# The shift's transfers issued from ScalarE's queue instead of SyncE's

## The reference

```python
xn = layernorm(x);  s = attn0(xn);  g = silu(ffn0(xn));  x = x + s * g    # ffn0: soft mixture, 8 experts, 64 slots each
xn = layernorm(x);  s = attn1(xn);  g = silu(ffn1(xn));  x = x + s * g    # ffn1: routed, 16 experts
# attention: 16 heads of 8, rotary q and k, causal
scores = einsum('bhqd,bhkd->bhqk', q, k) * 8 ** -0.5                      # masked above the diagonal
out = einsum('bhqk,bhkd->bhqd', softmax(scores), v)
```

## Time and profile before

| | us |
|---|---|
| median of 3 runs (lowest to highest) | 719.22 (716.24 to 719.84) |
| the profiled execution | 713.31 |
| its span, first to last instruction | 711.5 |
| busy: TensorE, VectorE, ScalarE, GpSimd | 616.2, 504.4, 455.0, 259.0 |

### The profile page before, as it was taken

The page is one execution under the profiler, slowest core; times in us unless marked ns, Lnnn a source line. Parts: engine busy times, 40 slices in busy tenths (PEclk is TensorE's granted clock), DMA queues, the critical chain, the costliest instruction groups (busy, mean ns, idle before and its releaser), DMA issues.

```text
span 711.5 us, 14086 instructions
## 1 busy us (share of the span) xinstructions
PE 616.2 (87%) x4988; PEld 293.0 (41%) x5052; DVE 504.4 (71%) x825; ACT 455.0 (64%) x908; POOL 259.0 (36%) x459
## 2 busy tenths in 40 slices
PE   0687399499988999999999999899999999999983
PEld 0455033245453555444352354432333333346632
DVE  7967588375775546888978978599988898843222
ACT  0463156266646688778766676687777777766781
POOL 5665021314300211687111106791132221116883
PEclk9788579799998999999999999999999999999997
DMA  5057431300551300306230444063331330200002
GB/s 175 0 180 156 125 121 40 68 1 31 139 156 41 71 28 4 95 23 189 75 91 18 81 116 126 2 180 125 71 85 33 80 67 18 53 2 1 1 0 60
DMA packets 33323, 52.09 MB, mean 73 GB/s; under 512 B 5832, under 2 KB 23912, under 8 KB 30696
## 3 DMA queue, kind: packets, MB, share of 16 engines
q1 hardware_dynamic: 31960, 50.74, 26.8%
q10 hardware_dynamic: 1296, 0.46, 0.2%
HBM read 37.29 MB, written 13.63 MB: 72 GB/s over the span
## 4 chain that ended last, share of the span: by engine, by line
PE 56%; DVE 13%; POOL 12%; ACT 6%; issue 6%; DMA 4%; SPq 2%; another core or an unknown queue 0%; POOLq 0%; ACTq 0%; DVEq 0%
PE ps L1319 52%; DVE maxes L1302 5%; ACT probs L1034 3%; DVE sine L1156 2%; POOL gate L550 2%; DMA qop<-shiftT 2%; SPq L736 2%; POOL probs L862 2%; PE ps L1534 1%; DMA F<-in_w 1%; POOL xn L550 1%; PE ps L1373 1%; POOL gate L907 1%; POOL gate L908 1%; POOL x L897 1%
## 5 line engine op out<-in xcount | busy, mean ns | idle before, releaser
L1302 DVE TENSOR_REDUCE maxes<-ps 128x2 f32<-128x1024 f32 (+2 forms) x288 | 338.6, 1220 | 91.1 <-PE ps L1319 89.5
L1034 ACT ACTIVATE probs<-ps 128x512 f32<-128x512 f32 x576 | 305.3, 605 | 110.0 <-PE ps L1319 68.5
L1319 PE MATMUL ps<-qop,kop 128*128 128x512 bf16 (+3 forms) x704 | 163.8, 327 | 22.4 <-DMA qop<-shiftT 9.3
L862 POOL TENSOR_SCALAR_AFFINE_SELECT probs<-probs 128x512 f32<-128x512 f32 (+1 forms) x160 | 83.8, 546 | 249.1 <-ACT probs L1034 249.1
L1319 PE MATMUL ps<-probs,vals 128*9 128x512 f32 (+3 forms) x1536 | 150.1, 493 | 4.9 <-POOL probs L862 3.1
L1319 PE MATMUL ps<-kmx,qmx 32*128 32x128 bf16 (+2 forms) x1280 | 101.9, 269 | 20.6 <-DMA qop<-shiftH 8.9
L1319 PEld LDWEIGHTS ps<-qop,kop 128*128 128x128 bf16 x768 | 60.2, 99 | 110.7 <-ACT probs L1034 50.0
L1319 PEld LDWEIGHTS ps<-kmx,qmx 32*128 32x128 bf16 x1280 | 38.1, 93 | 118.4 <-issue 66.4
L1319 PE MATMUL ps<-F 128*128 128x128 f32 (+2 forms) x640 | 76.9, 283 | 5.4 <-DMA F<-in_w 3.9
L1319 PEld LDWEIGHTS ps<-F 128*128 128x128 f32 (+2 forms) x640 | 69.2, 181 | 20.2 <-issue 16.3
L1319 PEld LDWEIGHTS ps<-probs,vals 128*9 128x9 f32 x1536 | 29.7, 90 | 60.5 <-issue 43.8
(11 more groups left out here) (158 smaller groups left out, 643.4 us busy)
## 6 DMA issues: line engine op xcount, KB each, us to landing
qop<-q_thirds SPq DMA_DIRECT2D x48, 192.0 KB
kop<-k_thirds SPq DMA_DIRECT2D x48, 192.0 KB
qmx<-q_thirds SPq DMA_DIRECT2D x16, 256.0 KB
kmx<-k_thirds SPq DMA_DIRECT2D x16, 256.0 KB
F<-in_w SPq DMA_DIRECT2D x16, 256.0 KB, 5.1
q_thirds<-third SPq DMA_DIRECT2D x8, 384.0 KB, 4.4
k_thirds<-third SPq DMA_DIRECT2D x8, 384.0 KB, 3.8
q_thirds<-third SPq DMA_DIRECT2D x8, 256.0 KB, 3.3
```

Source lines behind the costliest of these rows:

```text
L862: last = pool.affine_select(where, where, [[0, number], [1, P]], ALU.is_ge, 0.0, base=0, channel_multiplier=-1)
L1034: act.activation(probs[:, u % RING, :], bank(at), ACT.Exp, scale=SCALE).then_inc(s_cells_read, 1)
L1302: dve.tensor_reduce(dst, src, AX.X, ALU.max).then_inc(s_units_read[pair // 2], 1)
L1319: return pe.matmul(out_, lhsT, rhs, start=first, stop=last)
```

## The change

The branch for `shift` leaves SyncE's program. In ScalarE's it issues the same transfers, with the same source, destination and semaphore, after the copy; ahead of them ScalarE waits until its own copy is done (`s_cells_read`). The waits ahead of the copy are as before.

```diff
--- before.py
+++ after.py
@@ -759,16 +759,6 @@
                         sp.dma_start(qop[rows_i, r, :, :].rearrange("p h t -> p (h t)"), q_rows).then_inc(s_xload[r], 16)
                         sp.dma_start(kop[rows_i, r, :, :].rearrange("p h t -> p (h t)"),
                                      k_rows[D * i:D * i + 3 * D, :]).then_inc(s_xload[r], 16)
-                elif kind == "shift":
-                    n, part = arg
-                    sp.wait_ge(s_cells_read, CELL[what] + 1)
-                    if part == 2:
-                        for k in range(2):
-                            sp.dma_start(qop[KR + k:KR + k + 1, n % 2, :, :], shiftT[HG * TB * k:HG * TB * k + HG * TB, :]
-                                         ).then_inc(s_shift_in[k][n % 2], 16)
-                    else:
-                        sp.dma_start(qop[KR:KR + 2, n % 2, :, BANK * part:BANK * part + BANK], shiftH[:, part, :]
-                                     ).then_inc(s_shift_in[part][n % 2], 16)
                 elif kind == "ldw":
                     e, = arg
                     if e < 4:
@@ -1035,15 +1025,23 @@
                 elif kind == "shift":
                     n, part = arg
                     act.wait_ge(s_cells_full, CELL[what] + 1)
+                    r, last = n % 2, (n - 1) % 2
                     if n:
                         for half in range(2):
-                            act.wait_ge(s_shift_in[half][(n - 1) % 2], 16 * ((n - 1) // 2 + 1))
+                            act.wait_ge(s_shift_in[half][last], 16 * ((n - 1) // 2 + 1))
                     if part == 2:
                         act.activation(shiftT[:, :], bank(at)[0:2 * HG * TB, 0:P // 2].bitcast(BF16), ACT.Copy
                                        ).then_inc(s_cells_read, 1)
+                        act.wait_ge(s_cells_read, CELL[what] + 1)
+                        for k in range(2):
+                            act.dma_start(qop[KR + k:KR + k + 1, r, :, :], shiftT[HG * TB * k:HG * TB * k + HG * TB, :]
+                                          ).then_inc(s_shift_in[k][r], 16)
                     else:
                         act.activation(shiftH[:, part, :], bank(at)[0:2 * HG, 0:BANK // 2].bitcast(BF16), ACT.Copy
                                        ).then_inc(s_cells_read, 1)
+                        act.wait_ge(s_cells_read, CELL[what] + 1)
+                        act.dma_start(qop[KR:KR + 2, r, :, BANK * part:BANK * part + BANK], shiftH[:, part, :]
+                                      ).then_inc(s_shift_in[part][r], 16)
                 elif kind == "pvout":
                     n, half = arg
                     act.wait_ge(s_pv, summed(n, HALF_END[half]))
```

## The result

The changed kernel takes 721.2 us (median of 20 runs, 716.1 to 724.3), the kernel before beside it 716.7 us (20 runs, 713.6 to 720.0). The ratio is 1.007, 95% interval 1.0051 to 1.0089, so about 5.0 us slower. Forecast were 711.5 us and faster. The time lies inside the range (703 to 722), the direction is wrong.

A forecast was written before the change was run, and what follows sets the result against it. TensorE was taken to bound the kernel, with two shift-transfer stalls reachable. Gains of 7.0 + 7.4 + 0.8 = 15.2 us less 7.5 us on ScalarE gave -7.7 us: 719.2 to 711.5 us, range 703 to 722.

The forecast's parts named there:

- What bounds the kernel: TensorE sets the end; of its waits the change can reach only two, on the shift's transfers, 8.9 and 9.3 us.
- The two stalls: TensorE's waits for group 0's shiftH (8.9 us) and group 1's shiftT (9.3 us); with clock, 15.2 us to be gained.
- The landing beside a full queue: Shift transfers in ScalarE's queue take turns with SyncE's packets, adding 2.2 and 2.6 us to an undisturbed 1.9.
- First stall: Group 0, near 78 us: transfer issued at 74.8 instead of 80.17, landing at 79.2 instead of 86.23; 7.0 us gained.
- Second stall: Group 1, near 130 us: the pair lands at 129.6 instead of 137.02; 7.4 us gained, about 1.8 us waiting left.
- SyncE's queue: SyncE no longer stands at the shifts, so ready stores and loads can go earlier; effect on TensorE taken as zero.
- What it costs on ScalarE: Issues delay ScalarE's activations: six places at 0.95 us, six at 0.3, others nothing; 7.5 us lost.
- The clock: After the second stall TensorE's low clock costs 1.5 us; half recovered, 0.8 us, bounds -1.7 to +1.7.
- A: Stalls mostly stay: queues not served by turns, or ScalarE's issue held until SyncE's ends; +4.5 us, 715.5 to 723.7; chance 0.20.
- B: ScalarE comes to pace TensorE, its issue delays passing whole: 29 us against 15.2, +14 us, 733 us; chance 0.08.
- C: ScalarE's delay costs nothing and the stalls go whole: -16 to -19 us, 700 to 703 us; chance 0.14.
- D: The change does nothing because other work sets the pace behind the stalls; chance 0.06.

The follow-up runs named there:

- e8: Kernel before, SyncE issuing everything, with group 1's loads moved behind group 0's first shift and group 2's behind group 1's; ratio 0.9720, -20.1 us.
- e13: Kernel before with all shift transfers on ScalarE, SyncE held at each shift, and groups 1 and 2's loads waiting until the preceding shift's transfer landed; 0.9788, -15.2 us.
- e14: As e13, but only groups 0 and 1's shift transfers issued by ScalarE, the others by SyncE; ratio 0.9704 to the kernel before, -21.2 us.
- e1: Kernel before with only groups 0 and 1's shift transfers issued by ScalarE; ratio 0.9886, -8.2 us.
- e9: e1 with group 2's six loads cut into twelve, pieces of 1 KB instead of 8 KB; ratio 0.9896 to the kernel before, -7.5 us.
- e2: Kernel before with only group 8's shift transfers issued by ScalarE, SyncE not held; ratio 1.0091, +6.5 us.
- e6: Kernel before with only group 8's shift transfers issued by ScalarE, SyncE still waiting there for the copy; ratio 1.0024, +1.7 us.
- e4: The change with all transfers on ScalarE, but SyncE still waiting at each shift for the copy; ratio 0.9955 to the kernel before, -3.2 us.
- e3: Kernel before with only group 4's shift transfers issued by ScalarE, SyncE not held; ratio 1.0047, +3.4 us.
- e5: Kernel before with groups 9 to 15's shift transfers issued by ScalarE, SyncE held at those shifts; ratio 1.0061, +4.4 us.
- e12: Kernel before with groups 2, 3, 5, 6 and 7's shift transfers issued by ScalarE, SyncE held there; ratio 0.9982, -1.3 us.
- e11: e4 plus e8's order of loads, groups 1 and 2's behind the shifts; ratio 0.9955 to the kernel before, -3.2 us.

## Why the prediction was wrong

**What bounds the kernel: right.** The two stalls were the only waits that the change could take away, and they were worth more than I gave them: e8, which takes them both, gains 20 us.

**The landing beside a full queue: mis-sized, and the mechanism was wrong.** I priced it by turns of packets read at the start of the trace, 2.2 and 2.6 us on top of 1.9. First stall: 4.4 us expected from the end of the copy, 6.6 measured (75.77 to 82.33), near the far end of my bounds (6.1 to 7.0 us); TensorE's wait is 4.0 us where my sum left 1.3. Second stall: 4.5 us after the second issue expected, 8.8 measured; the wait shrank by 3.2 us, where my bounds began at 5. (The landing at 129.54 meets my 129.6 only because all of it stands 4.3 us earlier by then; TensorE's wait was to be about 1.8 us and is 6.1.) The issue while SyncE is stuck took 1.27 us, inside my bounds, but not because SyncE was stuck: the same issue takes 1.27 us in e13 and e14 too, where SyncE's issues ended over 1 us earlier. In all the term was to be 15.2 us and is 8.2 (e1), at the low end of my 8 to 19. The packets show the queues not taking turns (none of ScalarE's for 4.5 and 6.1 us), and in e9 a smaller piece didn't bring the landing forward; e13 and e14 show that 2.4 to 4.2 us is what such a transfer needs when the loads are held back (e13: 73.17 to 77.36 for group 0, 2.6 to 3.0 for group 1). The earlier trace rows had the queues side by side, but not the time of a small transfer under a full load; no row of before had it for a second queue, and I should have kept the 6 and 12 us that the rows do show as the likely value and not as the far end.

The Trainium skill, "DMA: Bandwidth & Descriptors", section "Issuing engines are not separate DMA queues", has the two engines' transfers interleave on the same 16 DMA engines, so that a second issuer saves only the issue. The runs agree in the main: 8.8 us against 12.4 us, where 2.8 was to be had. Its section "Queues, rings and completion order" also states that the count that reports a transfer lands only after every earlier write of that DMA engine, across its queues. I did not weigh this rule, and it spoke against the change. By the packets it is not what makes the transfers late here: at group 8 the ten packets themselves did not run for 6.1 of the 7.3 us, so a late count is at most the small rest. Why a queue has to wait so long for its turn no run here tells; that stays open.

**SyncE's queue, "I take zero": the step that turned the sign.** The prediction said that what is ready behind the shifts "can now go earlier" and stopped there. It asked whether TensorE waits for a group's load, and not what the earlier loads do to the transfer that they overtake. The wait at the shift was also what kept loads behind the shift. It costs 4.8 us at group 8 (e2 less e6, 1.9 to 7.7), 8.2 us between the change and e4 (6.3 to 10.2; 5.8 in their two traces). The row that would have warned was in hand: the earlier trace rows showed what six loads ahead of a shift do.

**What it costs on ScalarE: right in sum, not in place.** 7.5 us expected; 3.4 + 4.4 - 1.3 = 6.5 us from e3, e5 and e12, 8.2 with group 8's 1.7 (e6), which I had at nothing, and 6.0 (3.4 to 8.7) from e13 against e14. That the sum came out is partly luck: one place cost more than three times its price, and five cost nothing. Groups 9 to 15 were priced 4 x 0.95 + 3 x 0.3 = 4.7 us and measured 4.4. Group 4 was priced 0.95 and costs 3.4: the window of 3 us behind the copy showed ScalarE full, but not that it was full of work that empties no bank, and an issue took 1.35 us there. Groups 2, 3, 5, 6 and 7 were priced 1.9 us and cost nothing that can be told. The waits for `probs` went up by 7.0 us in the weight loads, as forecast, and by 6.4 more in the matmuls.

**The clock: wrong side.** I took back 0.8 us on the second stall. The clock still fell behind 6.1 us of waiting. It fell in a new place, behind 2.48 us at group 4, and behind 3.96 us at group 8 for 6.8 us where it had been low for 3.4.

**The rivals.** A came near in time (4.5 us slower) by a sum that is not what happened: it had the first stall's issue held, which it was not, and nothing gained at the second, where 3 us were. Its issue-lock half (the Trainium skill, "Perfetto Trace Analysis", section "DMA Instruction — HWDGE (DVE, Sync)") is not borne out: an issue of 1.27 us on ScalarE lay wholly inside one of SyncE's of 12.37 us. A's other half, pieces that wait for the other queue's, was nearer to what happened than my turns were. B's mechanism, ScalarE holding TensorE back, is there at group 4 and in groups 9 to 15, but costs 6.5 us in all where B had 29. C and D fall with e1: the stalls shrank, by 8.2 us, but went neither whole nor not at all. None of the rivals had the loads that overtake.

With what is known now the sum is -8.2 for the stalls, + 6.5 for ScalarE (group 8's 1.7 aside), + 1.7 + 4.8 for group 8, that is +4.8 us, give or take 4.6.

## What to carry to other kernels

A wait in an issuing engine's program also keeps the transfers behind it back; before it is taken away, list what goes out earlier and which small, urgent transfer it will overtake. For such a transfer order matters more than the engine that issues it: in one queue ahead of the loads it was quick (e8, 2.8% faster than before), while a second queue beside the loads brought 1.1%. When an issue goes to a computing engine, look at what stands behind it that frees no buffer, such as a table load, since there the delay has no cover.

## What the hardware showed that I had not expected

- A pair of 8 KB transfers took 1.9 us undisturbed, 2.4 to 3.0 us just ahead of six loads, 8.7 to 9.7 us in the other queue behind them (the change, e1, e4), and 11.6 to 13.1 us in the same queue behind them (before and seven runs that leave group 1 on SyncE). Pieces of 1 KB instead of 8 KB in the loads made the last landing 8.6 us.
- A small transfer in ScalarE's queue moved no packet for 4.5 us (group 0) and 6.1 us (group 8) while SyncE's queue moved 303 and 212.
- ScalarE's issue of a small transfer is mostly 0.5 to 0.7 us, but single ones took 1.27 us (group 0's first, whether SyncE was stuck or issued nothing) and 1.35 us (group 4, with SyncE issuing nothing near it); no row shows why.
- SyncE's longest issue of a store of `k_thirds` took 10.48 us before and 12.37 us after the change, and 1.50 us when the six loads ahead of these stores were moved (e8; 1.7 to 3.7 us in e11, e13 and e14).
- Behind TensorE's wait at group 4 the granted clock fell to the lower level for 6.8 us in two traces (waits of 2.48 us in the change, 2.60 in e4), for 3.4 us in e13's (2.18), and not at all in e3's (2.61) and e11's (2.2).
